# A mixture of experts computed on its chosen rows instead of on every row, in a one-core kernel of attention, experts and a gated delta rule

## What is computed

```
FFN(xn):                                    # causal attention, then experts
  a   = rmsnorm(xn) ; 16 heads of 128, causal softmax, output projection
  hid = xn + attention(a)
  x2  = rmsnorm(hid) * ln2                  # 1024 rows of 256
  p   = softmax(x2 @ gate_w.T)              # 16 experts
  w   = the 4 largest p of a row, divided by their sum; 0 for the other 12 experts
  routed = sum over e of w[:, e] * (silu(x2 @ G_e) * (x2 @ U_e)) @ D_e    # inner width 176
  shared = (silu(x2 @ G_s) * (x2 @ U_s)) @ D_s                            # inner width 352
  return hid + routed + shared
GDN(xn):                                    # chunked gated delta rule, 16 key heads, 32 value heads
```

## Time and profile before

| | us |
|---|---|
| median of 3 runs (1761.71 to 1766.79) | 1762.07 |
| the profiled execution | 1764.03 |
| its span, first to last instruction | 1762.2 |
| PE busy | 1672.9 (95%) |
| DVE busy | 1113.1 (63%) |
| ACT busy | 766.2 (43%) |
| POOL busy | 372.2 (21%) |

### The profile page before, as it was taken

How to read it: one execution, slowest core, us unless ns; L and a number is a source line. 1 busy time by engine, 2 the same in 40 slices (tenths; PEclk the granted TensorE clock), 3 DMA queues, 4 the chain that set the end, 5 groups by cost and what they waited for, 6 DMA issues and landing times.

```text
span 1762.2 us, 28367 instructions
## 1 busy us (share of the span) xinstructions
PE 1672.9 (95%) x11094; PEld 1134.6 (64%) x11094; DVE 1113.1 (63%) x2369; ACT 766.2 (43%) x1597; POOL 372.2 (21%) x207
## 2 busy tenths in 40 slices
PE   5999999998899999876999999999999999999987
PEld 4566666666455555534687668766876676677666
DVE  4554445543612222246788988898888888888875
ACT  3544444444201111044555645564556455645551
POOL 0000000000000000052315431543253325332510
PEclk9999999999799999986999999999999999999999
DMA  3111111110011111041333233313331333233210
GB/s 106 36 48 43 30 49 48 49 42 12 6 45 32 32 36 36 16 132 46 66 76 77 52 86 77 74 50 86 82 70 49 91 82 66 53 91 82 58 14 31
DMA packets 194010, 99.35 MB, mean 56 GB/s; under 512 B 158435, under 2 KB 167907, under 8 KB 193878
## 3 DMA queue, kind: packets, MB, share of 16 engines
q1 hardware_dynamic: 193878, 97.54, 21.8%
HBM read 84.66 MB, written 8.65 MB: 53 GB/s over the span
## 4 chain that ended last, share of the span: by engine, by line
PE 49%; issue 43%; DVE 4%; ACT 1%; DMA 1%; SPq 1%; POOLq 1%; POOL 0%; DVEq 0%; ACTq 0%
PE ps L664 6%; PE ps L765 6%; PE ps L683 6%; PE ps L602 3%; PE ps L704 3%; PE ps L735 3%; PE ps L612 3%; PE ps L714 2%; PE ps L734 2%; PE ps L691 2%; PE ps L818 2%; PE ps L634 2%; PE ps L643 2%; PE ps L671 2%; PE ps L811 1%
## 5 line engine op out<-in xcount | busy, mean ns | idle before, releaser
L550 PE MATMUL ps<-xrT,w 128*128 128x512 f32 x400 | 182.3, 601 | 1.1 <-DMA w<-in_w 1.1
L1089 ACT ACTIVATE vs<-ps 128x256 f32<-128x256 f32 x128 | 49.1, 383 | 262.8 <-PE ps L704 258.4
L1717 POOL TENSOR_TENSOR qg<-qT,Ebc 128x1024 f32<-128x1024 f32 x32 | 75.0, 2364 | 393.2 <-PE ps L735 393.2
L1346 DVE TENSOR_TENSOR su<-ps,sg 128x512 f32<-128x512 f32 x44 | 30.4, 691 | 191.9 <-PE ps L550 191.9
L1297 DVE TENSOR_TENSOR ps<-ps,causal_neg 128x128 f32<-128x128 f32 x128 | 37.4, 292 | 164.6 <-PE ps L452 164.6
L1429 DVE SCALAR_TENSOR_TENSOR cv<-ps,cw,cv 128x1022 f32<-128x1022 f32 (+2 forms) x96 | 122.6, 1279 | 25.4 <-ACT cv L1036 21.5
L1027 ACT ACTIVATE sg<-ps 128x512 f32<-128x512 f32 x50 | 29.9, 597 | 250.2 <-PE ps L550 247.4
L664 PE MATMUL ps<-xnT,gv 128*128 128x512 f32 x256 | 120.9, 616 | 11.9 <-DVE cv L1429 11.4
L765 PE MATMUL ps<-wout,xT 128*128 128x256 f32 x512 | 127.2, 392 | 2.2 <-DVE total L1539 2.2
L550 PEld LDWEIGHTS ps<-xrT,w 128*128 128x128 f32 x400 | 77.1, 193 | 79.6 <-issue 76.0
L1440 DVE SCALAR_TENSOR_TENSOR cv<-ps,cw,cv 128x1022 f32<-128x1022 f32 (+2 forms) x96 | 122.5, 1277 | 5.7 <-ACT cv L1068 3.4
(11 more groups left out here) (219 smaller groups left out, 3543.5 us busy)
## 6 DMA issues: line engine op xcount, KB each, us to landing
dec<-grow_dram SPq DMA_DIRECT2D x32, 512.0 KB, 5.2
Ebc<-erow_dram SPq DMA_DIRECT2D x32, 512.0 KB, 4.9
wqk<-in_wqk SPq DMA_DIRECT2D x16, 512.0 KB, 3.8
w<-in_w SPq DMA_DIRECT2D x25, 256.0 KB, 2.7
wv<-in_wv SPq DMA_DIRECT2D x16, 256.0 KB, 2.6
wo<-in_wo SPq DMA_DIRECT2D x16, 256.0 KB, 2.7
gkq<-in_gkq SPq DMA_DIRECT2D x16, 256.0 KB, 2.7
gv<-in_gv SPq DMA_DIRECT2D x16, 256.0 KB, 2.7
```

What stands on the lines that cost most here:

```text
L550: last = mm(ps[:, bank, :], w13[:, j % 3, k, part * P:(part + 1) * P], xrT[:, k, n * 512:(n + 1) * 512], start=(k == 0), stop=(k == HK - 1))
L1717: tt(qg[:, r], qT[:], Ebc[:, r], ALU.mult).then_inc(fl["g_qg"], 1)
```

## The change

Only the stage of the experts is computed differently; pieces of it are placed in the two other stages.

- **Routing by halves.** The rows of sequence 0 are complete after attention iteration 7. ACT squares them at the end of iteration 8 (`row_squares`), POOL makes their scales, DVE scales them at the end of 9 (`scaled_rows`), PE turns them in 9 (`turn_rows`, 8 transposes), multiplies them by the router's weights in 10 (`route`, 8 matmuls) and counts them in 12 (`count_rows`, 4 matmuls); DVE ranks in 11 and makes row numbers in 12. Sequence 1 has the same steps after the last iteration, between the shared expert's units.
- **Scatter.** POOL sends each row of `x2` to four places of a table in DRAM, `xs_dram`, one part of 1024 rows for each expert: 16 indirect DMAs for each half (`send_rows`). The table is zeroed first: SP issues two 1 MB stores after `wo`'s load in each of the iterations 0 to 7, and in iterations 8 to 15 the loads of one expert's weights (352 KB and 176 KB) in the same place. The other eight experts are loaded when the last iteration has read the probabilities, whose memory they take.
- **The shared expert** alone runs as before, as 6 units over all rows (padded from 352 to 384 inner columns), without `token_weights`.
- **47 slots.** A slot is a tile of 128 rows of one expert. 4096 chosen rows in tiles that each belong to one expert make at most 47. DVE works out which expert and which tile of the table each slot has. SP reads a tile's number into a register and loads the tile, six slots ahead. PE reads the slot's expert into a register, three slots ahead, and addresses the resident weights by it. A slot is 2 transposes, 2 matmuls of 352 columns, 2 transposes, and 2 matmuls of 256 columns over 88 rows; ACT moves the turned rows, takes the silu and moves the result, DVE multiplies and moves the turned product, SP stores the result in `ys_dram`.
- **Gather.** In the first eight heads of the delta rule POOL fetches 4 x 128 rows of results for each head (`expert_rows`, at the end of its iteration) and DVE adds them into `total`, weighted (`add_experts`, four instructions between `residuals(h, 1)` and `states(h, 1)`).

The core of the diff:

```
+                if k < 8:                       # SP, at the end of attention iteration k
+                    clear_rows(2 * k)           # 1 MB of zeros to xs_dram, each
+                    clear_rows(2 * k + 1)
+                else:
+                    load_expert(k - 8)
+            sp.wait_ge(sm["s_pv"], 4 * PAIRS)
+            for e in range(E // 2, E):
+                load_expert(e)
+            def load_rows(s):
+                if s >= RING:
+                    sp.wait_ge(sm["m_x"], s - RING + 1)
+                tile = sp.value_load(slot_tile[0:1, s:s + 1], min_val=0, max_val=E * CAP // P)
+                rows = xs_dram.rearrange("(q p) h -> p q h", p=P)[:, bass.DynSlice(tile, 1), :]
+                dma(xs[:, s % RING, :], rows.rearrange("p q h -> p (q h)")).then_inc(rows_in[s % RING], 16)
+            def store_rows(s):
+                sp.wait_ge(sm["m_yE"], s + 1)
+                dma(ys_dram[s * P:(s + 1) * P], yg[:, s % 4, :]).then_inc(rows_out[s % 4], 16)
+            sp.wait_ge(sm["r_rows"], 7)
+            sp.wait_ge(sm["m_scat"], 16 * TOPK * NT)
...
+            gate_and_up(0)                      # PE, after the last attention iteration
+            gate_and_up(1)
+            turn_rows(1, 6)
+            down(0)
+            route(1, 6)
+            gate_and_up(2)
+            down(1)
+            gate_and_up(3)
+            count_rows(1, 7)
+            gate_and_up(4)
+            down(2)
+            gate_and_up(5)
+            pe.wait_ge(sm["r_rows"], 5)
+            for u in range(SHT, 2 * SHT):
+                down(u)
...
+            def expert_of(s):
+                return pe.value_load(slot_expert[0:1, s:s + 1], min_val=0, max_val=E - 1)
+            def slot_gate_and_up(s, e):
+                pe.wait_ge(sm["m_xE"], s + 1)
+                if s >= 2:
+                    pe.wait_ge(sm["m_h"], s - 1)
+                for k in range(HK):
+                    last = mm(ps[:, s % 2, 0:2 * I], xsT[:, s % 3, k, :], expert_weights(we13[:], e, k),
...
+            pe.wait_ge(sm["m_we"], 32 * E)
+            pe.wait_ge(sm["r_rows"], 7)
+            experts = [expert_of(s) for s in range(3)]
+            turn_slot(0)
+            turn_slot(1)
+            for s in range(SLOTS + 2):
+                if s < SLOTS:
+                    slot_gate_and_up(s, experts[s])
+                if s + 2 < SLOTS:
+                    turn_slot(s + 2)
+                if s + 3 < SLOTS:
+                    experts.append(expert_of(s + 3))
+                if s >= 2:
+                    slot_down(s - 2, experts[s - 2])
+                if 1 <= s <= SLOTS:
+                    turn_hidden(s - 1)
...
+                for t in range(4 * b, 4 * b + 4):      # POOL, send_rows(b)
+                    for j in range(TOPK):
+                        pool.indirect_dma_start(out=xs_dram, out_offset=bass.IndirectOffsetOnAxis(ap=place[:, t, j:j + 1], axis=0),
+                                                in_=x2[:, t, :], in_offset=None).then_inc(sm["m_scat"], 16)
...
+            def add_experts(i):                 # DVE, in heads 0 to 7
+                for a in range(4):
+                    t, j = i % 2 * 4 + a, i // 2
+                    dve.wait_ge(sm["m_got"], 64 * (i + 1))
+                    stt(total[:, t, :], yg[:, a, :], pick[:, t, j:j + 1], total[:, t, :], ALU.mult,
+                        ALU.add).then_inc(sm["m_used"], 1)
```

More of the change, by code:

```diff
@@ L512, in _ @@
                     scores(k + 1, 1)
[L514 to L522, removed]
@@ L542, in gate_and_up @@
[L542 to L552, removed]
@@ L554, in token_weights @@
[L554 to L576, removed]
-                                    ws[:, t].rearrange("p a e -> p (a e)"), ident[:])
-                if t % 4 == 3:
-                    last.then_inc(sm["r_wT"], 1)
-            pe.wait_ge(sm["r_wTE"], 2)
-            for u in range(EARLY):
-                token_weights(u)
@@ new lines, in down @@
+            def down(u):
+                j, n = u % SHT, u // SHT
+                if u == 0:
+                    pe.wait_ge(sm["f_ld"], 32 * SHT)
+                pe.wait_ge(sm["f_act"], u + 1)
+                for t in range(4 * n, 4 * n + 4):
+                    last = mm(ps[:, 4 + t // 2, (t % 2) * H:(t % 2 + 1) * H], act_t[:, j, t * P:(t + 1) * P],
+                              w2[:, j, :], start=(j == 0 and t % 2 == 0), stop=(j == SHT - 1), skip_group_check=True)
+                last.then_inc(sm["f_dn"], 1)
@@ new lines, in turn_hidden, with slot_down @@
+            def turn_hidden(s):
+                pe.wait_ge(sm["m_h"], s + 1)
+                if s < 2:
+                    pe.wait_ge(sm["f_hid"], 4)
+                if s >= 2:
+                    pe.wait_ge(sm["m_tE"], s - 1)
+                for k in range(2):
+                    last = pe.transpose(ps[0:IH, 4 + s % 2, k * P:(k + 1) * P], hs[:, s % 2, k * IH:(k + 1) * IH], ident[:])
+                last.then_inc(sm["m_t"], 1)
+            def slot_down(s, e):
+                pe.wait_ge(sm["m_tE"], s + 1)
+                if s >= 2:
+                    pe.wait_ge(sm["m_yE"], s - 1)
+                for k in range(2):
+                    last = mm(ps[:, 6 + s % 2, 0:H], hsT[:, s % 2, k, :], expert_weights(we2[0:IH], e, k),
+                              start=(k == 0), stop=(k == 1))
+                last.then_inc(sm["m_y"], 1)
@@ new lines, in take_output @@
+            def take_output(s):
+                act.wait_ge(sm["m_y"], s + 1)
+                if s >= 4:
+                    act.wait_ge(rows_out[s % 4], 16 * (s // 4))
+                fn(yg[:, s % 4, :], ps[:, 6 + s % 2, 0:H], ACT.Copy).then_inc(sm["m_yE"], 1)
+            take_slot(0)
+            take_slot(1)
+            for s in range(SLOTS + 2):
+                if s < SLOTS:
+                    slot_silu(s)
+                if s + 2 < SLOTS:
+                    take_slot(s + 2)
+                if s >= 2:
+                    take_output(s - 2)
@@ L1410, in _ @@
-            for i in range(4):
-                rows = total[:, 2 * i:2 * i + 2, :].rearrange("p t h -> p (t h)")
-                tt(rows, ps[:, 4 + i, :], rows, ALU.add)
+            places(1, 7)
+            up_times_gate(4)
+            expert_starts()
+            up_times_gate(5)
+            slots()
+            for n in range(4):
+                dve.wait_ge(sm["f_dn"], SHT if n < 2 else 2 * SHT)
+                rows = hid[:, 2 * n:2 * n + 2, :].rearrange("p t h -> p (t h)")
+                tt(rows, ps[:, 4 + n, :], rows, ALU.add).then_inc(sm["f_hid"], 1)
@@ L1413, in _ @@
+            for s in range(SLOTS + 1):
+                if s < SLOTS:
+                    slot_hidden(s)
+                if s >= 1:
+                    take_hidden(s - 1)
             section_end(dve)
```

613 lines of the change are left out of this document (402 added, 211 removed).

## The result

The changed kernel takes 1692.8 us (median of 4 runs, 1688.3 to 1696.0) beside 1764.4 (median of 4, 1761.7 to 1769.0) for the kernel before: 0.959 of it, 95% interval 0.9557 to 0.9622. That is 71.6 us less, where 24 were forecast. The time lies inside the range, the direction is as forecast, and the gain is three times as large. The profiled execution took 1692.8 us and has a span of 1691.0; it is 71.2 us shorter than that of the kernel before.

What follows compares the result with a forecast made beforehand. The prediction took PE's instruction stream to bound the kernel. The delta rule starting 88 us earlier (-88) and attention's +64.5 gave -24 on 1764.0, so 1740 us; the range was 1690 to 1800, the forecast's own 1715 to 1770.

Steps and rivals of the forecast that it cites:

- Attention, forecast +64.5: Attention stage: 55 us for `wqk` behind the zeroing stores, 3.5 behind experts' loads, 6 of added PE work.
- Eight long waits: Attention iterations 0 to 7: PE stands 5.2 us each for `wqk`'s load behind two 1 MB stores.
- The lower clock: Attention, after each long `wqk` wait: idle PE falls to half clock, costing 1.7 us more.
- Rival B: Attention: the clearing is hidden, transfers interleave or `wqk` overtakes; 16 or 0 instead of 55 us, about 1690; chance 0.11.
- The shared expert, forecast 42.1 us of PE: After attention: six dense units 33.6 us, 8 transposes 1.0, 8 router matmuls 3.5, 9 counting matmuls 4.0.
- The gap and the scatter: Before the first slot: PE idles 14 us while POOL issues 16 indirect DMAs at 1.3 each, 21 us.
- Rival D: POOL's indirect DMAs cost 2.9 us: +26 before the slots, up to +36 in the heads, 1766 to 1802; chance 0.08.
- The slots, forecast 3.4 us: Experts' stage: 2.66 us of PE work plus 0.75 exposed register load per slot; 47 slots take 160 us.
- The upper bound: Register load in a slot: 1.8 us wholly exposed, the shortest round trip of a transfer shown.
- Rival A: Slots: PE's queue is deep enough to hide the register load; 2.7 us a slot, 33 less, 1707; chance 0.13.
- The delta rule, forecast 0: Delta rule's first eight heads: gathers and DVE's additions lie in existing waits and cost nothing.
- Rival E: Slots: PE's clock stays at half after 14 us of idling; 125 us more, about 1860; chance 0.06.

Runs made afterwards that it cites:

- Experiment 1: Changed kernel with SP issuing the zeroing stores and the experts' loads behind `wv`'s load, not ahead of `wqk`'s: 1632.8 us, ratio 0.926.
- experiment 2: Changed kernel with one of the two 1 MB zeroing stores issued behind `wv`'s load, the other left ahead of `wqk`'s: 1663.3 us, ratio 0.943.
- experiment 3: Changed kernel with the zeroing stores issued from POOL's queue at the same moment, experts' loads left on SP ahead of `wqk`: 1650.0 us, ratio 0.936.
- experiment 9: Changed kernel with 8 instead of 16 indirect DMAs in sequence 1's scatter, so rows reach two of four experts: 1679.8 us, ratio 0.953.
- experiment 6: Changed kernel with PE reading each slot's expert into a register twice instead of once: 1695.1 us, ratio 0.961.
- experiment 7: Changed kernel with PE reading each slot's expert into a register three times instead of once: 1718.4 us, ratio 0.975.
- experiment 8: Changed kernel without `expert_rows` and `add_experts`, so the routed experts' results are not added to the output: 1692.4 us, ratio 0.959.
- experiment 4: Changed kernel with slot s using expert s // 3 by a fixed address, without register loads: 1689.1 us, ratio 0.959.

## Why the prediction came out as it did

**Attention, forecast +64.5, measured 502.1 - 437.0 = +65.1.** The mechanism and the sum hold. Eight long waits were forecast at 5.2 us and cost 4.0 to 5.5, 4.44 as a mean (35.5 in all). Two errors of the sum partly cancel in it. The stores' transfer was put at 6.3 us, and `wqk` lands only 4.1 later (7.9 for 3.8 in most of the eight); but SP takes 1.3 us to issue the two stores, which the sum left out: 4.1 + 1.3 - 1.0 = 4.4. (The slack of 1.0 goes by the median landing of 3.8; the very load of the earlier trace rows landed after 4.3.) The lower clock was forecast at 1.7 each. It was 1.6 to 1.7 in six and 2.4 and 3.1 in the other two; L502's group grew by 134.8 - 117.8 = 17.0 us, or 2.1 each: 52.5 for 55. The iterations with experts' loads pay 5.7 for 3.5. PE's added work is 4.0 for 6, because the router's matmuls took 0.23 each and not 0.44. The smaller rest is 3: L479's and L606's matmuls, the same as before, grew by 2.0 together. Experiment 1 takes 60 back, all but the added work and a wait or two. Rival B did not come about: in SP's queue `wqk` waited for the stores. Experiments 2 and 3 show why the forecast's picture holds. The wait shrinks by 2.5 us with each megabyte taken from in front of `wqk`, and it is gone or small in six of eight iterations with both of them in flight beside it in another queue. With the rule of ring order in the Trainium skill (DMA: Bandwidth & Descriptors, Queues, rings and completion order) these traces agree, with 2.5 us a megabyte and a landing of 4.7 beside the stores in POOL's queue.

**The shared expert, forecast 42.1 us of PE, measured 538.1 - 502.1 = 36.0.** The step that failed is "8 router matmuls (3.5) and 9 counting matmuls (9 x 0.44 = 4.0)". The price came from a row whose 16 matmuls ran at a clock of 0.50. In the middle of dense work the eight took 1.85 us and the nine 2.2. I had both rows side by side and did not correct the one by the other. That is 3.5 of the 6.1 us. The 33.6 of the dense units hold (32.6 by their groups); the last 1.7 are overlaps of one group's end with the next one's start, which the sum did not have. POOL's first scatter instruction, too, came 25.3 us after attention (527.35) and not 30.

**The gap and the scatter, forecast 14 us, 1.3 for each indirect DMA, first slot 56 us after attention; measured 14.6, 1.27 and 50.6.** The bounds were 0.43 and 2.9, so the choice within them was largely luck; experiment 9 shows that this price, times the number of indirect DMAs, is what the gap grows by. Rival D had no ground.

**The slots, forecast 3.4 us, measured 2.49: the step that failed most.** The text put it as "I take 0.75: the load is a round trip, but of one word, and half a microsecond of matmuls is in the queue." 47 x 0.75 = 35 us. Both halves were off. The load is not the round trip of a transfer, but 0.47 us of the sequencer (0.6 with the gaps). What is covered is not half a microsecond but about 1.1 by the same records (experiments 6 and 7). The upper bound was built on the landing time of a DMA of 128 KB, which a read of one word doesn't resemble, and I chose a value towards the middle of a span that this row had made wide. The Trainium skill (DMA: Bandwidth & Descriptors, Latency and other measured facts) has a floor of about 600 ns for a register load. The trace has 301 ns for the load itself; only with its arithmetic, its check and the gaps between them is it 0.6 us. The estimate from that page took the load as exposed, too. The other 0.17 is PE's own work, 2.49 for 2.66: 8 us over 47 slots. The pitches in the trace are 1.19 + 0.22 + 0.86 + 0.22, where the sum had 1.24 + 0.26 + 0.90 + 0.26. Rival A is the case that came about, and it gave 1707.

**What is left over.** From the gap to the end of the slots 165 us were forecast, and it was 122.3 (552.7 to 675.0). Shared expert -6.1, gap and attention +1.3, slots -42.7: -47.5 beside the forecast's -24 is -71.5, and -71.6 was measured by the medians, -71.2 between the two profiled executions.

**The delta rule, forecast 0.** It runs 1010.7 us from its first projection to the end, beside 1010.3, and experiment 8 gives nothing when the gathers are left out. **Rival E** had no ground either: the mean clock was 0.50 from 553 to 557, 0.82 to 561 and 1.00 from there on.

The forecast's range for a slot said that under 2.9 the prediction is wrong. By that it was, in the slots; the rest of the sum held to a few microseconds.

## What to carry to other kernels

A bulk transfer "hidden" in a stage where the DMA engines are a tenth busy is paid for when it stands in front of a load that has a microsecond of slack. Put it behind the last load that something waits for, or on another engine's queue. A register that addresses weights costs its engine's sequencer time and no wait at all, as long as the register work between matmuls stays under what is covered there, here about 1.1 us in a slot of 2.49; double it in a trial to see the margin. Before a duration is carried over from a row, look at the clock that the row ran at.

## What the runs showed of the hardware

- About 1.1 us of register work of PE's sequencer is hidden in a slot of 2.49 us: 1.12 is (experiment 6), 1.59 shows 0.52 (experiment 7).
- Reading one word of SBUF into a register of PE takes 301 ns, and 151 and 18 more for the arithmetic and the bounds, 0.6 us from start to end; a register in an address costs 46 ns for each matmul (changed kernel).
- An indirect DMA of 128 rows of 1 KB costs POOL 1.27 us (changed kernel), and a plain store of 1 MB issued by POOL 0.86 (experiment 3).
- The length of a wait of PE does not tell by itself whether the clock falls. Behind waits for `wqk` of 2.17 and 2.28 (experiment 2) and 2.25 us (experiment 7) the projection ran in part at the lower level, 5.40 us. Behind 2.52 (experiment 2), 2.84 (experiment 3) and 3.00 (experiment 4) it kept its 3.70 us at full clock. Behind all those of 3.35 us and more it did not. What tells the shorter ones apart stays open.
